# A four-layer graph transformer on one core: scatters in fours over both rankings, stages joined by chunks, and a finer wait in the sum pass

## The chip, the cores and the metric

The kernel runs on one core of one Trainium2 chip. The metric is the device time of one execution in microseconds (us). Tensors are fp32 unless marked bf16.

## The reference

The input is a graph of 3125 nodes with 256 features and 50,000 edges. Each of four layers is a graph part, a linear or softmax attention part and a mixture of experts, added to `x`. What the change touches is this, in short:

```python
# linear attention (layers 0 and 3), per head of 32 columns
q, k = elu(x @ Wq) + 1, elu(x @ Wk) + 1
ctx, den = k.T @ (x @ Wv), k.sum(nodes)             # "context"
msg = (q @ ctx) / (q @ den) @ Wo

# graph part of layer 2
agg = segment_sum(msgs[src, rel], dst)              # "sum pass"
i, f, g, o = split(agg @ W_ih.T + b_ih + b_hh)
hn = sigmoid(o) * tanh(sigmoid(i) * tanh(g))
x += relu(relu(hn @ W1.T + b1) @ W2.T + b2) @ W3.T + b3

# graph part of layer 3: this twice, with 4 heads and an elu behind it, then with 1
xW = x @ W                                          # a row per node, "table"
e = leaky_relu((xW * a_src).sum(head)[src] + (xW * a_dst).sum(head)[dst])
out = segment_softmax(e, dst) weighted sum of xW[src], + bias
```

## The kernel before

The 3125 nodes are 25 tiles of 128 (`NT`), the edges are 400 tiles of 128 (`ET`) in 50 batches of 8 (`SB`). Activations lie transposed in SBUF as `x[128, 2, 3200]`; dense work goes over them in 8 chunks of 400 columns (`CW`, `NC`), work by rows in the 25 tiles. The program is a row of stages. At the end of each all engines meet at a barrier. Inside a stage each engine has an instruction stream of its own, in the order of the code; semaphores tie them (`wait_ge`, `then_inc`).

**`rank`, the first stage.** It sorts the edges by destination (order 0, "dst") and then by source (order 1, "src"). For each order it prepares one-hot matrices, and then its ranking loop runs over 50 batches: PE counts and picks (the semaphore `chosen[o]` says how many batches it has picked, plus 2), ACT copies the counts and forms differences of keys, DVE compares and sums (its first instruction on the picks is line 318), and every second batch DVE writes the destinations of 16 edge tiles (`placed`, line 338). POOL scatters each edge tile of order 0 to DRAM with one indirect DMA, 400 in all (`scatter_slots`, line 499): 8 of a batch as soon as its two batches are placed. Order 1's 400 scatters (line 518) are spread over later stages of layer 0, beside other work: `beside=lambda pool: later.some(pool, 3)` issues three for each step.

**Small stages.** `turn_rows` (`L0_add`, `L2_turn`, `L3_h_turn`, `L3_add`) transposes 25 tiles of rows on PE and adds or copies them into `x`. `layers` and `gates` run dense layers by chunks; `context` goes over 25 tiles with key and value products, an elu and an outer product. `rows_of` makes the table of layer 3: for each tile 4 matmuls give 256 columns in PSUM; DVE copies them to a row, multiplies them with `a_src` and `a_dst` and reduces three times (lines 3780 to 3787), and SP stores the row. `finish_softmax` (`L3a_finish`, `L3b_finish`) joins the own edge of each node to the sums in `acc` on DVE, with operations over all 25 tiles. `flow` is a stage of several units that go over the chunks one behind another: in step `i` each engine does, unit by unit, the chunk `i - lag` of the unit.

**The sum pass of layer 2 (`L2_edges`).** 52 batches of 8 edge tiles. POOL gathers 128 rows for each tile (line 676) into a ring of 4 batches (`RING`), PE multiplies them with a one-hot matrix (line 688, semaphore `summed`), DVE adds the result to `acc` (line 728, `merged`); ACT makes the one-hot matrices. The softmax attention of layer 2 runs beside it. POOL waits before each batch:

```python
if n >= RING:
    pool.wait_ge(summed, (n - RING + 1) * SB)
```

## Time and profile before

| | us |
|---|---|
| median of 3 runs (7988.39 to 7998.42) | 7996.3 |
| the profiled execution, its own time | 7963.28 |
| its span | 7961.3 |
| `rank` | 996.7 |
| `L0_add`, queries, context | 144.9 |
| `L2_edges` | 701.6 |
| `L2_turn`, `L2_gates`, `L2_head` | 142.5 |
| `L3_norm`, context of layer 3 | 132.6 |
| `L3a_table` | 61.6 |
| `L3a_finish`, `L3_h_turn`, `L3_elu`, `L3b_table` | 126.7 |
| `L3b_finish`, `L3_add`, `L3_norm2` | 115.1 |

PE is TensorE, with its weight loads apart as PEld; DVE is VectorE, ACT ScalarE, POOL GpSimd, SP the engine that issues direct DMAs. The stages named are cut at their barriers; the mean clock granted to TensorE over the span is 0.812 of full speed. A busy share over the whole program says little here, since the stages have different limits.

### The profile page before, as it was taken

How to read it: one execution, taken by the hardware profiler on the slowest of the kernel's cores; microseconds unless marked ns; L12 is line 12 of the kernel's file. 1: busy time of each engine (PE TensorE's matmuls, PEld its weight loads, DVE VectorE, ACT ScalarE, POOL GpSimd, SP SyncE). 2: the span in 40 equal slices, each digit the busy share in tenths (PEclk: the TensorE clock that was granted, in tenths of full speed). 3: DMA queues.
4: the chain of work that ended last, by engine and by line, in shares of the span. 5: the costliest groups of instructions: out<-in, count | busy, mean ns of one | idle time of the engine just before them, and what ended most of it. 6: DMA issues, size and time to landing. Idle time of an engine off the chain costs nothing. (4 is left out here: it accounts for less than half of the span.)

```text
span 7961.3 us, 86418 instructions
## 1 busy us (share of the span) xinstructions
PE 5473.5 (69%) x21790; PEld 3563.2 (45%) x21790; DVE 3893.7 (49%) x9476; ACT 2872.1 (36%) x7916; POOL 3239.0 (41%) x3257
## 2 busy tenths in 40 slices
PE   2222535566799777776894668799858866888767
PEld 1111323334455455554463344555545543555544
DVE  5335835554311389994543323412456675545611
ACT  4223627774122144440112333122246642555211
POOL 3664035553466256661005652200056633555211
PEclk9999966668799878887997778699856656788588
DMA  2221521111010255550012321100034333333222
GB/s 81 66 66 40 181 71 39 41 40 17 26 33 20 70 156 159 159 146 16 8 35 86 85 82 40 39 33 30 15 101 108 106 69 86 93 88 93 56 91 86
DMA packets 270423, 568.85 MB, mean 71 GB/s; under 512 B 85678, under 2 KB 136802, under 8 KB 263906
## 3 DMA queue, kind: packets, MB, share of 16 engines
q0 software_dynamic: 134496, 314.63, 15.8%
q1 hardware_dynamic: 135554, 249.89, 9.6%
q8 instruction: 155, 2.54, 0.1%
q14 instruction: 218, 1.79, 0.1%
HBM read 519.26 MB, written 45.00 MB: 71 GB/s over the span
## 5 line engine op out<-in xcount | busy, mean ns | idle before, releaser
L1291 POOL DMA_INDIRECT L_edges_rows<-scratch_L_kv,L_edges_index x416 | 521.1, 1253 | 312.3 <-PE L_edges_ps_sum L1567 186.2
L1291 POOL DMA_INDIRECT L3a_edges_rows<-scratch_L3a,L3a_edges_index x416 | 442.9, 1065 | 446.8 <-DMA L3a_edges_last<-order_dst_last 216.5
L1291 POOL DMA_INDIRECT L3b_edges_rows<-scratch_L3b,L3b_edges_index x416 | 397.5, 955 | 465.0 <-PE L3b_edges_ps_sum L1567 302.0
L1291 POOL DMA_INDIRECT L_edges_rows<-scratch_L,L_edges_index x416 | 410.6, 987 | 320.2 <-DVE L_edges_msg L1338 176.7
L499 POOL DMA_INDIRECT scratch_by_dst<-dst_record,dst_dest x400 | 414.6, 1036 | 303.8 <-DVE dst_dest L338 185.5
L1745 POOL TENSOR_TENSOR L_norm_u_half<-x 128x400 f32<-128x400 f32 x64 | 70.8, 1109 | 1135.2 <-DVE x L1845 626.3
L676 POOL DMA_INDIRECT L_edges_rows<-scratch_L,L_edges_index x416 | 394.9, 949 | 325.1 <-PE L_edges_ps_sum L688 135.9
L518 POOL DMA_INDIRECT scratch_by_src<-src_record,src_dest x400 | 387.7, 969 | 255.1 <-issue 107.6
L688 PE MATMUL L_edges_ps_sum<-L_edges_rows,L_edges_hot 128*128 128x256 f32 x832 | 268.4, 464 | 220.4 <-issue 101.3
L400 PE MATMUL rank_ps_count<-rank_parts,rank_ident_b 128*128 128x225 bf16 x200 | 53.6, 370 | 530.9 <-DVE rank_parts L312 457.0
L1432 DVE TENSOR_TENSOR L_acc<-L_edges_ps_sum,L_acc 128x264 f32 (+1 forms) x832 | 360.0, 433 | 112.8 <-DVE L_acc L1432 56.6
L2788 DVE TENSOR_TENSOR L_experts_gated_h<-L_experts_hidden,L_experts_share_rows 128x800 f32<-128x800 f32 x112 | 111.1, 993 | 619.5 <-ACT L_experts_hidden L2778 583.8
L2778 ACT ACTIVATE L_experts_hidden<-L_experts_ps_h,L_eb_sb 128x400 f32<-128x400 f32 x320 | 187.9, 594 | 619.9 <-PE L_experts_ps_h L2740 473.1
L1567 PE MATMUL L3a_edges_ps_sum<-L3a_edges_rows,L3a_edges_hot 128*128 128x264 f32 x832 | 379.5, 618 | 0.7 <-DVE L_acc L1432 0.7
L728 DVE TENSOR_TENSOR L_acc<-L_edges_ps_sum,L_acc 128x256 f32 x416 | 176.7, 425 | 385.6 <-DMA L_edges_last<-order_src_last 196.9
L2751 PE MATMUL L_experts_ps_o<-L_experts_gated_h,L_e_sb 128*128 128x400 f32 x896 | 337.1, 518 | 29.0 <-DVE L_experts_gated_h L2788 29.0
L464 ACT ACTIVATE rank_apart<-x,rank_key_f 128x128 bf16<-128x128 f32 x800 | 244.4, 388 | 300.0 <-remote 226.7
L1567 PE MATMUL L3b_edges_ps_sum<-L3b_edges_rows,L3b_edges_hot 128*128 128x258 f32 x832 | 337.2, 557 | 4.3 <-DVE L_acc L1432 4.2
L1567 PE MATMUL L_edges_ps_sum<-L_edges_rhs,L_edges_hot 128*128 128x264 f32 x832 | 335.9, 553 | 5.5 <-DVE L_acc L1432 1.9
L2740 PE MATMUL L_experts_ps_h<-xn,L_e_sb 128*128 128x400 f32 x896 | 323.6, 505 | 2.1 <-PEq L113 2.1
L1666 ACT ACTIVATE L_edges_rhs<-L_edges_msg,L_edges_rhs 128x64 f32<-128x64 f32 x1248 | 306.6, 334 | 27.5 <-issue 21.6
L688 PEld LDWEIGHTS L_edges_ps_sum<-L_edges_rows,L_edges_hot 128*128 128x128 f32 x832 | 175.1, 227 | 307.9 <-issue 148.7
(762 smaller groups left out, 13309.7 us busy)
## 6 DMA issues: line engine op xcount, KB each, us to landing
x<-scratch_dst_key_rows SPq DMA_DIRECT2D x50, 512.0 KB
x<-scratch_src_key_rows SPq DMA_DIRECT2D x50, 512.0 KB
L_experts_w<-in_L_w SPq DMA_DIRECT2D x16, 1024.0 KB
L_edges_rows<-scratch_L,L_edges_index POOLq DMA_INDIRECT x832
L_edges_lo_rows<-order_src_lo_rows SPq DMA_DIRECT2D x52, 256.0 KB
L3a_edges_lo_rows<-order_dst_lo_rows SPq DMA_DIRECT2D x52, 256.0 KB
L3b_edges_lo_rows<-order_dst_lo_rows SPq DMA_DIRECT2D x52, 256.0 KB
x<-scratch_dst_lo_rows SPq DMA_DIRECT2D x50, 256.0 KB
```

The source lines that it names most:

```text
L464: ins = nc.scalar.activation(apart[:, u, k, :], key_line[:, u, k * P:(k + 1) * P], ACT.Abs, scale=-1.0, bias=key_f[:, ds(n * SB + k, 1)])
L499: pool.indirect_dma_start(order["table"], bass.IndirectOffsetOnAxis(order["dest"][:, t:t + 1], 0), order["record"][:, t, :], None).then_in ...
L518: pool.indirect_dma_start(self.order["table"], bass.IndirectOffsetOnAxis(self.order["dest"][:, t:t + 1], 0), self.order["record"][:, t, :] ...
L676: pool.indirect_dma_start(rows[:, n % RING, k, :], None, row_table, bass.IndirectOffsetOnAxis(index[:, t:t + 1].bitcast(U32), 0)).then_inc ...
L688: nc.tensor.matmul(ps_sum[:, k % 4, 0:F], hot[:, n % RING, k, :], rows[:, n % RING, k, :], start=True, stop=True).then_inc(summed, 1)
L1291: pool.indirect_dma_start(rows[:, n % RING, k, 0:RW], None, row_table, bass.IndirectOffsetOnAxis(index[:, t:t + 1].bitcast(U32), 0)).then_ ...
L1432: v.tensor_tensor(a, ps_sum[:, (c * SB + k) % BANKS, 0:M], a, ALU.add).then_inc(merged, 1)
L1567: nc.tensor.matmul(ps_sum[:, (c * SB + k) % BANKS, 0:M], hot[:, c % RING, k, :], values(c)[:, k, :], start=True, stop=True).then_inc(summe ...
L1666: ins = nc.scalar.activation(out, src, ACT.Copy, scale=parts(c)[:, k, h, V:V + 1])
L2740: ins = nc.tensor.matmul(ps_h[:, (a + o) % 4, 0:CW], weights[l][:, e, f, o * P:(o + 1) * P], r, start=f == 0, stop=f == len(src) - 1)
L2751: nc.tensor.matmul(ps_o[:, o, 0:CW], weights[hid][:, e, f, o * P:(o + 1) * P], gated_h[:, n % 2, f, :], start=e == 0 and f == 0, stop=False)
L2778: nc.scalar.activation(hidden[l][:, n % 2, o, :], ps_h[:, a % 4, 0:CW], func, bias=biases[l][:, n % EX, o:o + 1]).then_inc(taken, 1)
```

## The change

1. `scatter_slots` issues the 400 scatters of order 0 four at a time, one group behind each of the 100 ranking batches of both orders, where it waits for `chosen[o]`.
2. In the sum pass POOL waits for `summed` before each tile, for the tile that held the same place in the ring.
3. Layer 0: transpose and add, queries and context are one `flow`; three scatters of order 1 for each of the 25 tiles stand beside it, where 24 and 50 stood.
4. Layer 2: transpose, gates and the three dense layers are one `flow`.
5. Layer 3: norm, queries and context are one `flow`.
6. The tables of layer 3: the scores come as 8 (or 2) further columns of the matmul, whose weights are formed once from `W` and `a` (`ScoreColumns`); DVE has three copies for each tile.
7. `L3a_finish`, transpose, elu and the second table are one `flow`: `Finish` works tile by tile, and its own rows are loaded in 8 pieces.
8. `L3b_finish`, transpose, add, norm and rows are one `flow`.

```diff
-                scatter_slots(pool, orders[0], scattered, placed[0])
...
+                scatter_slots(pool, orders[0], scattered, placed[0], chosen)
...
+def scatter_slots(pool, order, scattered, placed, chosen):
...
-    for n in range(rounds):
-        if placed is not None and n % 2 == 0:
-            pool.wait_ge(placed, n // 2 + 1)
-        if n >= 4:
-            pool.wait_ge(scattered[n % 4], n // 4 * (16 * SB))
-        for k in range(SB):
-            t = n * SB + k
-            pool.indirect_dma_start(order["table"], bass.IndirectOffsetOnAxis(order["dest"][:, t:t + 1], 0),
-                                    order["record"][:, t, :], None).then_inc(scattered[n % 4], 16)
+    portion = SB // 2
+    for o in range(2):
+        for n in range(rounds):
+            pool.wait_ge(chosen[o], n + 3)
+            first = (o * rounds + n) * portion
+            b = first // SB
+            if first % SB == 0:
+                if b % 2 == 0:
+                    pool.wait_ge(placed, b // 2 + 1)
+                if b >= 4:
+                    pool.wait_ge(scattered[b % 4], b // 4 * (16 * SB))
+            for t in range(first, first + portion):
+                pool.indirect_dma_start(order["table"], bass.IndirectOffsetOnAxis(order["dest"][:, t:t + 1], 0),
+                                        order["record"][:, t, :], None).then_inc(scattered[b % 4], 16)
...
-                    if n >= RING:
-                        pool.wait_ge(summed, (n - RING + 1) * SB)
                     for k in range(SB):
                         t = n * SB + k
+                        if n >= RING:
+                            pool.wait_ge(summed, (n - RING) * SB + k + 1)
                         pool.indirect_dma_start(
                             rows[:, n % RING, k, :], None, row_table,
                             bass.IndirectOffsetOnAxis(index[:, t:t + 1].bitcast(U32), 0)).then_inc(gathered[n % RING], 16)
...
         for t in begun(i - self.lag):
+            to = self.x[:, :, t * P:(t + 1) * P]
+            got = self.ps[:, t % self.depth, 0:2 * P].rearrange("p (f n) -> p f n", f=2)
+            if self.how == "elu":
+                dve.wait_ge(self.lowered, t + 1)
+                for f in range(2):
+                    ins = v.tensor_scalar(to[:, f], got[:, f], self.bias[:, f:f + 1], 0.0, ALU.add, ALU.max)
+                ins.then_inc(self.floored, 1)
+                dve.wait_ge(self.floored, t + 1)
+                dve.wait_ge(self.raised, t + 1)
+                v.scalar_tensor_tensor(out=to, in0=self.power[:, t % 2], scalar=-1.0, in1=to, op0=ALU.add,
+                                       op1=ALU.add).then_inc(self.taken, 1)
...
+class Finish:
...
+        for t in begun(i):
+            dve.wait_ge(self.weighed, t + 1)
+            if H > 1 and t >= self.RING:
+                dve.wait_ge(self.reader.turned, t - self.RING + 1)
+            for h in range(H):
+                ins = v.scalar_tensor_tensor(out=self.out(t)[:, h * (V - 1):(h + 1) * (V - 1)],
+                                             in0=acc[:, t, h * V:h * V + V - 1],
+                                             scalar=fall[:, 0, t, h:h + 1], in1=self.own[:, t, h * V:h * V + V - 1],
+                                             op0=ALU.mult, op1=ALU.add)
+            ins.then_inc(self.finished, 1)
...
+class ScoreColumns:
...
+    def tensor(self, pe, i):
...
+            for o in range(2):
+                ins = self.nc.tensor.matmul(self.ps[:, f, :], self.w_rows[:, o, f * P:(f + 1) * P], self.a_heads[:, o, :],
+                                            start=o == 0, stop=o == 1)
+        ins.then_inc(self.made, 1)
+
...
+class Context:
...
+    def pool(self, pool, i):
+        for t in self.mine(i) if self.beside else ():
+            pool.wait_ge(self.made, t + 1)
+            self.beside(pool)
...
+            if t >= 2:
+                pe.wait_ge(self.taken, t - 1)
+            for w, at_ in ((self.wk, 0), (self.wv, D)):
+                for f in range(2):
+                    ins = self.nc.tensor.matmul(self.ps[:, t % 2, at_:at_ + D], self.src[:, f, t * P:(t + 1) * P], w[:, f, :],
+                                                start=f == 0, stop=f == 1)
+            ins.then_inc(self.made, 1)
+            if t >= 1:
+                self.outer(pe, t - 1)
...
     attention_out(kit, f"{name}_out", q, ctx, den, spread, wo, dst, floor, plus, shrink, bias, besides[1])


...
         (wq, wk, wv, wp, bp, spread), mix_in = m.room("L0_wq", "L0_wk", "L0_wv", "L0_wp", "L0_bp", "spread")
-        turn_rows(kit, "L0_add", rows, x, add=True, loads=mix_in)
-        q = m("L0_mix_q", [P, 2, NP])
-        layers(kit, "L0_mix_queries", [Layer(wq, xn, q, func="elu1")], beside=lambda pool: later.some(pool, 3))
-        linear_attention(kit, "L0_mix", m, xn, q, wk, wv, wp, spread, x, 1e-6, 0.0, 1.0, bias=bp,
-                         besides=(lambda pool: later.some(pool, 2), lambda pool: later.some(pool, 6)))
+        linear_attention(kit, "L0_mix", m, [TurnIn(rows, x, 0, None)], xn, wq, wk, wv, wp, spread, x, 1e-6, 0.0, 1.0, bias=bp,
+                         loads=mix_in, besides=(lambda pool: later.some(pool, 3), lambda pool: later.some(pool, 6)))
...
-                turn_rows(kit, "L2_turn", acc, agg, loads=gates_in + head_in)
                 hn = m2("L2_hn", [P, 2, NP])
-                gates(kit, "L2_gates", agg, wih, bih, hn)
-                h1, h2 = m2("L2_head_h1", [P, 1, CW]), m2("L2_head_h2", [P, 1, CW])
-                layers(kit, "L2_head", [Layer(w1, hn, h1, bias=b1, func="relu"), Layer(w2, h1, h2, bias=b2, func="relu"),
-                                        Layer(w3, h2, x, bias=b3, add=True)])
+                turned = TurnIn(acc, agg, 0, None, how="copy", depth=2)
+                gates = Gates(wih, bih, agg, hn, 1, turned)
+                first = Dense([(w1, agg[:, 1:2, :], b1)], hn, 2, gates, func="relu", banks=1)
+                second = Dense([(w2, agg[:, 0:1, :], b2)], agg[:, 1:2, :], 3, first, func="relu", banks=1)
+                third = Dense([(w3, x, b3)], agg[:, 0:1, :], 4, second, func="add", banks=1)
+                flow(kit, "L2_head", [turned, gates, first, second, third], loads=gates_in + head_in)
...
                 nc.vector.tensor_copy(row[:, 0:F].rearrange("p (h v) -> p h v", h=heads)[:, :, 0:V - 1],
                                       banks[0][:, 0:D].rearrange("p (h v) -> p h v", h=heads))
-                nc.vector.tensor_tensor(prod[:, 0, :], banks[0][:, 0:D], a_src, ALU.mult)
-                link(nc.vector.tensor_tensor(prod[:, 1, :], banks[0][:, 0:D], a_dst, ALU.mult))
-                both = prod[:].rearrange("p a (h v) -> p (a h) v", h=heads)
-                nc.vector.tensor_reduce(row[:, F:F + heads], both[:, 0:heads], X, ALU.add)
-                nc.vector.tensor_reduce(s_src[:, ds(t, 1), :].squeeze(1), both[:, 0:heads], X, ALU.add)
-                return nc.vector.tensor_reduce(s_dst[:, ds(t, 1), :].squeeze(1), both[:, heads:2 * heads], X, ALU.add)
...
-            rows_of(kit, f"{name}_table", [(src, w, D)], finish, sink=sink, setup=setup)
+                nc.vector.tensor_copy(row[:, F:F + heads], banks[0][:, D:D + heads])
+                return nc.vector.tensor_copy(both[:, t, :], banks[0][:, D:D + 2 * heads])
+
+            def sink(sp, t, r, u, extra):
+                return sp.dma_start(node_rows(table, t), extra["row"][:, u, :])
+
+            columns = ScoreColumns(w_rows, a_heads, w[:, :, D:])
+            units, src, loads = ahead(m2, weights_in)
+            flow(kit, f"{name}_table", units + [columns, Rows([[(src, w, D + 2 * heads)]], finish, 2 if units else 0,
+                                                              units[-1] if units else None, sink=sink, setup=setup, depth=3,
+                                                              columns=columns)], loads=loads)
...
-        finish_softmax(kit, f"{name}_finish", acc, heads, V, acc[:, :, 0:D], own_score=own, own_dram=table)
...
             norm = Norm(x, xn, after=skip)
-            flow(kit, "L3_norm", [skip, norm, Dense([(wq, q, None)], xn, 2, norm, func="elu1")], loads=mix_in,
-                 loads_later=weights_in + biases_in)
-            linear_attention(kit, "L3_mix", m3, xn, q, wk, wv, wm, spread, msg, -3e38, 1e-6, float(N))
-        return xn
+            linear_attention(kit, "L3_mix", m3, [skip, norm], xn, wq, wk, wv, wm, spread, msg, -3e38, 1e-6, float(N),
+                             normed=True, loads=mix_in, loads_later=weights_in + biases_in)
+        return [], xn, []
...
     with Memory(kit) as m:
         acc = m("L3_acc", [P, NT, 264])
         rows = acc[:, :, 0:D]
-        attend(kit, "L3a", 1, 4, first, order, scratch["L3a"], acc)
+        own = m("L3a_own", [P, NT, 4]), m("L3b_own", [P, NT, 1])
...
-        attend(kit, "L3b", 2, 1, between, order, scratch["L3b"], acc, lambda s: MessageMlp(kit, s, xn, msg, x))
-        turn_rows(kit, "L3_add", rows, x, add=True, bias=gb2)
+            finish = Finish(acc, 4, 65, own[0], scratch["L3a"])
+            finish.reader = TurnIn(None, h, 1, finish, how="elu", bias=gb1)
+            return [finish, finish.reader], h, weights_in
+
+        attend(kit, "L3b", 2, 1, between, order, scratch["L3b"], acc, own[1], lambda s: MessageMlp(kit, s, xn, msg, x))
+        given = msg.rearrange("p f n -> p (f n)").rearrange("p (t d) -> p t d", t=NT)
...
+            (gw,), gate_in = m2.room("L3_gw")
...
+            turned = TurnIn(rows, x, 1, done, bias=gb2, depth=2)
+            skip = AddIn(x, xn, bias=out_b, lag=2, after=turned)
+            norm = Norm(x, xn, lag=5, after=skip)
+            flow(kit, "L3_norm2", [done, turned, skip, norm,
+                                   Rows([[(xn, gw, EXPERTS), (xn, None, D)]], finish, 7, norm, depth=3),
+                                   Blank(scratch["given"][0:EXPERTS * CAPT * P, :])],
+                 loads=gate_in + bias_in)
     with Memory(kit) as m:
```

POOL, the scatters of `rank` (the name in brackets is the semaphore waited for). Before, at its start:

```order
L499 DMA scratch_by_dst<-dst_record,dst_dest 54448x8 x15
L499 DMA scratch_by_dst<-dst_record,dst_dest 54448x8 [waits rank_placed0]
L499 DMA scratch_by_dst<-dst_record,dst_dest 54448x8 x15
L499 DMA scratch_by_dst<-dst_record,dst_dest 54448x8 [waits rank_scattered0,rank_placed0]
L499 DMA scratch_by_dst<-dst_record,dst_dest 54448x8 x7
```

Now, where POOL passes from order 0's batches to order 1's:

```order
L504 DMA scratch_by_dst<-dst_record,dst_dest 54448x8 [waits rank_chosen0]
L504 DMA scratch_by_dst<-dst_record,dst_dest 54448x8 x3
L504 DMA scratch_by_dst<-dst_record,dst_dest 54448x8 [waits rank_scattered1,rank_chosen1]
L504 DMA scratch_by_dst<-dst_record,dst_dest 54448x8 x3
L504 DMA scratch_by_dst<-dst_record,dst_dest 54448x8 [waits rank_chosen1]
L504 DMA scratch_by_dst<-dst_record,dst_dest 54448x8 x3
```

Runs of 16 and 8 have become runs of 4, each behind a wait, and half of them stand beside order 1.

DVE, the second table of layer 3 (`L3b_table`; `ps` is PSUM). Before, one tile:

```order
L3780 COPY L3b_table_row<-L3b_table_ps 128x256
L3782 TENSOR_TENSOR L3b_table_prod<-L3b_table_ps,L_as_sb 128x256
L3783 TENSOR_TENSOR L3b_table_prod<-L3b_table_ps,L_ad_sb 128x256
L3785 TENSOR_REDUCE L3b_table_row<-L3b_table_prod 128x1
L3786 TENSOR_REDUCE L3b_ssrc<-L3b_table_prod 128x1
L3787 TENSOR_REDUCE L3b_sdst<-L3b_table_prod 128x1
```

Now, the end of one step of the joined stage and the start of the next (`u_rows` are the finished rows, `u_power` the exponentials of the elu):

```order
L2117 TENSOR_SCALAR L_h<-L3b_table_u_ps,L_gb_sb 128x128 x2
L2121 SCALAR_TENSOR_TENSOR L_h<-L3b_table_u_power,L_h 128x2x128
L4076 COPY L3b_table_row<-L3b_table_u_ps 128x256
L4078 COPY L3b_table_row<-L3b_table_u_ps 128x1
L4079 COPY L3b_both<-L3b_table_u_ps 128x2
...
L2282 SCALAR_TENSOR_TENSOR L3b_table_u_rows<-L_acc,L3b_table_u_fall,L3b_table_u_own 128x64 x12
L2117 TENSOR_SCALAR L_h<-L3b_table_u_ps,L_gb_sb 128x128 x2
```

The finish of one chunk (12 operations for three tiles), the turn and elu of the chunk before and the table rows of the one before that now stand in one DVE stream without a barrier between them.

## Rows read from the trace of the kernel before

**Rows 1.** The page: span, and busy time of each engine (x instructions).
```profile
span 7961.3 us, 86418 instructions
...
PE 5473.5 (69%) x21790; PEld 3563.2 (45%) x21790; DVE 3893.7 (49%) x9476; ACT 2872.1 (36%) x7916; POOL 3239.0 (41%) x3257
```

**Rows 2.** Windows of `rank`: stretch and length, busy us of the engines, clock, DMA.
```profile
8.80:96.00 87.20, 22.26 (x430) 17.21 (x431) 75.15 (x363) 54.38 (x150) 0.00 (x0) 1.00 0.25 79
96.00:676.00 580.00, 123.30 (x1288) 82.35 (x1286) 185.94 (x447) 134.39 (x435) 381.77 (x367) 1.00 0.22 66
676.00:790.00 114.00, 22.50 (x434) 17.49 (x434) 74.28 (x351) 53.40 (x150) 32.80 (x34) 1.00 0.08 25
790.00:1005.50 215.50, 122.78 (x1285) 82.17 (x1282) 181.56 (x448) 134.54 (x434) 0.00 (x0) 1.00 0.54 172
```

**Rows 3.** Waits, 96 to 676: total us, how many, longest us.
```profile
DVE x L318 <- remote: 335.2, 21, 26.7
...
POOL scratch_by_dst L499 <- DVE dst_dest L338: 185.5, 12, 105.2
```

**Rows 4.** Timeline of POOL: start us, duration us, instruction, idle time before it.
```profile
307.17 0.97 POOL L499 DMA_INDIRECT scratch_by_dst<-dst_record,dst_dest  x1 [6.72 <-DVE dst_dest L338]
...
349.04 0.97 POOL L499 DMA_INDIRECT scratch_by_dst<-dst_record,dst_dest  x1 [0.30 <-issue]
356.99 0.97 POOL L499 DMA_INDIRECT scratch_by_dst<-dst_record,dst_dest  x1 [6.99 <-DVE dst_dest L338]
```

**Rows 5.** Timeline of DVE in the same stretch.
```profile
323.80 0.57 DVE L318 TENSOR_TENSOR x<-rank_ps_pick,xn 128x400 f32<-128x400 f32 x1 [4.52 <-issue]
...
353.67 0.57 DVE L318 TENSOR_TENSOR x<-rank_ps_pick,xn 128x400 f32<-128x400 f32 x1 [26.20 <-remote]
```

**Rows 6.** Windows: `L0_add`, queries, context; then `L3_norm` and the context of layer 3.
```profile
1881.00:1900.60 19.60, 14.66 (x50) 7.29 (x50) 12.11 (x50) 0.00 (x0) 10.00 (x25) 0.50 0.31 107
1900.60:1942.30 41.70, 26.89 (x64) 12.83 (x64) 9.19 (x16) 16.65 (x32) 23.08 (x24) 0.91 0.02 2
1942.30:2025.90 83.60, 61.82 (x304) 51.61 (x304) 21.16 (x58) 19.45 (x50) 47.98 (x50) 0.93 0.02 2
...
5520.30:5589.10 68.80, 52.71 (x208) 33.74 (x208) 33.96 (x48) 39.90 (x60) 18.33 (x16) 0.83 0.11 39
5589.10:5652.90 63.80, 58.27 (x304) 52.00 (x304) 21.36 (x58) 20.02 (x50) 0.00 (x0) 0.94 0.00 1
```

**Rows 7.** Windows: the three stages of layer 2 (4898.9 on), and `L3a_table`.
```profile
4898.90:5041.40 142.50, 117.87 (x322) 60.30 (x322) 48.36 (x99) 43.92 (x64) 9.95 (x25) 0.88 0.03 8
...
5718.50:5780.10 61.60, 36.93 (x100) 22.29 (x100) 54.47 (x151) 0.00 (x0) 0.00 (x0) 0.74 0.16 55
```

**Rows 8.** Windows: `L3a_finish` to `L3_elu`; `L3b_table`; `L3b_finish` with `L3_add`; `L3_norm2`.
```profile
6498.70:6563.80 65.10, 16.11 (x50) 7.26 (x50) 54.43 (x79) 6.00 (x3) 10.00 (x25) 0.50 0.19 59
6563.80:6625.40 61.60, 37.02 (x100) 22.70 (x100) 54.44 (x151) 0.00 (x0) 0.00 (x0) 0.75 0.16 54
7456.40:7504.90 48.50, 15.95 (x50) 7.34 (x50) 37.51 (x64) 0.24 (x1) 10.00 (x25) 0.52 0.21 68
7504.90:7571.50 66.60, 60.47 (x294) 53.15 (x294) 39.87 (x90) 10.18 (x17) 18.61 (x17) 0.55 0.16 64
```

**Rows 9.** The sum pass, `L2_edges`: its window.
```profile
4197.30:4898.90 701.60, 415.96 (x1392) 285.23 (x1392) 243.56 (x565) 237.15 (x580) 394.87 (x416) 0.77 0.29 79
```

**Rows 10.** The sum pass: waits of POOL.
```profile
POOL L_edges_rows L676 <- PE L_edges_ps_sum L688: 135.9, 26, 7.9
POOL L_edges_rows L676 <- issue: 117.8, 385, 0.5
```

**Rows 11.** The sum pass: timeline of POOL over one cycle of two batches.
```profile
4324.27 0.95 POOL L676 DMA_INDIRECT L_edges_rows<-scratch_L,L_edges_index  x1 [6.80 <-PE L_edges_ps_sum L688]
...
4343.23 0.95 POOL L676 DMA_INDIRECT L_edges_rows<-scratch_L,L_edges_index  x1 [0.30 <-issue]
4350.96 0.94 POOL L676 DMA_INDIRECT L_edges_rows<-scratch_L,L_edges_index  x1 [6.78 <-PE L_edges_ps_sum L688]
```

More of the change, by code:

```diff
@@ L1887, in tensor @@
                 pe.wait_ge(*self.loaded)
-            if o == 0:
+            if o == 0 and self.after:
                 self.after.ready(pe, c)
@@ L1935, in open @@
         self.nc, self.kit, self.loaded = kit.nc, kit, loaded
-        self.ps = [s.ps(f"{name}ps{j}", [P, self.depth, 512]) for j in range(len(self.parts[0]))]
+        self.widths = [n for _, _, n in self.parts[0]]
+        self.one_bank = sum(self.widths) <= 512
+        self.ps = [s.ps(f"{name}ps{j}", [P, self.depth, 512]) for j in range(1 if self.one_bank else len(self.widths))]
         self.made, self.taken, self.chain = (s.sem(f"{name}{n}") for n in ("made", "taken", "chain"))
@@ L1939, in open, with bank @@
         self.extra = self.setup(s) if self.setup else None
+    def bank(self, j, k):
+        if not self.one_bank:
+            return self.ps[j][:, k % self.depth, :]
+        at_ = sum(self.widths[:j])
+        return self.ps[0][:, k % self.depth, at_:at_ + self.widths[j]]
     def mine(self, i):
@@ L1968, in tensor @@
             for j, (src, w, n) in enumerate(self.parts[r]):
[L1969 removed]
+                to = self.bank(j, k)
                 for f in range(src.shape[1]):
@@ L3083, in linear_attention @@
-def linear_attention(kit, name, m, xn, q, wk, wv, wo, spread, dst, floor, plus, shrink, bias=None, besides=(None, None)):
+def linear_attention(kit, name, m, ahead, xn, wq, wk, wv, wo, spread, dst, floor, plus, shrink, bias=None, normed=False,
+                     loads=(), loads_later=(), besides=(None, None)):
+    q = m(f"{name}_q", [P, 2, NP])
     ctx, den = m(f"{name}_ctx", [P, 2, D]), m(f"{name}_den", [P, 2, DEN + HEADS * NC])
-    context(kit, f"{name}_context", xn, wk, xn, wv, 2, ctx, True, den=den, scale=1.0 / shrink, beside=besides[0])
+    normed, lag = (ahead[-1], ahead[-1].last + 1) if normed else (None, 0)
+    flow(kit, f"{name}_context",
+         ahead + [Dense([(wq, q, None)], xn, lag, normed, func="elu1"),
+                  Context(xn, wk, wv, ctx, den, 1.0 / shrink, lag, normed, besides[0])], loads, loads_later)
@@ L3758, in layer2, with attend @@
         experts(kit, "L2_experts", xn, x, [e1, e2], [eb1], eb2, comb_t, scratch["shares"], ACT.Gelu)
-def attend(kit, name, j, heads, src, order, table, acc, guest=None):
+def attend(kit, name, j, heads, ahead, order, table, acc, own, guest=None):
     nc = kit.nc
@@ L3855, in layer3 @@
         rows = acc[:, :, 0:D]
[L3856 removed]
+        own = m("L3a_own", [P, NT, 4]), m("L3b_own", [P, NT, 1])
+        attend(kit, "L3a", 1, 4, first, order, scratch["L3a"], acc, own[0])
         def between(m2, weights_in):
             h = m2("L3_h", [P, 2, NP])
[L3860 to L3864 removed]
```

397 lines of the change are left out of this document (294 added, 103 removed).

## The prediction

> **What bounds the kernel now.** I read the page first: PE is busy 69% of the span and no engine more [rows 1], so no single engine is the limit. The windows cut at the barriers then give each stage its own limit. The reader should look there for two things. In `rank` the same work stands twice: the ranking loop of order 0 takes 580.0 us, that of order 1 215.5 us, with the same busy times on PE (123.3 and 122.8), DVE (185.9 and 181.6) and ACT (134.4 and 134.5) and the clock at 1.00 in both [rows 2]. The only difference is POOL, which scatters in the first and not in the second. So some 364 us of waiting come with 400 scatters. In the small stages the busiest engine fills 70 to 95% of a stage that is 20 to 85 us long, and the rest is fill, drain and a clock of 0.50 to 0.56 where PE has little to do [rows 6 to 8].
>
> The waits name the loss in `rank`: DVE's first instruction on PE's picks waits 335.2 us for "remote", 21 times, up to 26.7 us, and POOL waits 185.5 us for destinations [rows 3]. The timeline shows how: POOL scatters 32 tiles back to back from 307.17 to 349.04 + 0.97 = 350.01 and then waits 6.99 us [rows 4]; DVE's line 318 comes at 323.80 after an idle time of 4.52 us, which began at 323.80 - 4.52 - 307.17 = 12.1 us into the run, and the next one at 353.67 after 26.20 us, only 3.7 us after the last scatter has ended [rows 4, 5]. So for some 12 us of a run the other engines keep their pace, then they nearly stand, and 3.7 us after POOL stops they go on. POOL itself is limited to one scatter in 1.28 us: 32 in 42.8 us, and a few of them longer [rows 4].
>
> **Rank (part 1).** The 400 scatters stay, so POOL still has 400 x 1.28 = 512 us of them. A group of four is 5.1 us, a ranking batch alone 215.5 / 50 = 4.3 us. So POOL is now the slower of the two, and both loops go at its pace or slower. How much slower is not in the trace, for no run of four stands there. From below: 5.1 us a batch, 510 for both loops. From above: the disturbance per scatter stays what it is, 364.5 / 400 = 0.91 us, and the loops take 2 x 215.5 + 364.5 = 795.5, as now. POOL can run at most about two groups ahead, since each waits for a batch picked; after some 12 us of scatters the other engines slow, no pick comes, POOL stops, and they recover in up to 3.7 us. I take that as a cycle of three batches, 15.3 us of scatters and 2.5 us of stop, 17.8 / 3 = 5.9 us a batch, 590 for 100. A second estimate agrees: with scatters beside it a tile of `context` takes 83.6 / 25 = 3.34 us and without 63.8 / 25 = 2.55, which is 0.40 us for each of 50 scatters [rows 6]; 431 + 400 x 0.40 = 591. So the loops lose 795.5 - 590 = 205 us. Order 1's preparation takes 114.0 us with scatters still draining into it (34 of them), order 0's takes 87.2 without [rows 2]; now at most one group is left there: -27. The last groups come behind order 1's last picks and must land: +8. Sum **-224**, bounds -304 (5.1 us a batch) and about -19 (nothing but the gap).
>
> The Trainium skill, SBUF — State Buffer, section "Who interferes with whom", says that PE and ACT never wait on anyone and that a DMA never contends with a compute engine. By it there would be no disturbance for a new schedule to remove, and `rank` would gain the gap alone; this trace does not agree, with 580.0 against 215.5 us for equal work.
>
> **Joined stages (parts 3 to 8).** For each I take the busiest engine over the joined windows, PE's at a better clock where it had been starved, plus some 5 us of ends (the context of layer 3 takes 63.8 for 58.3 of PE [rows 6]). The upper bound of each is today's time, for the work is nearly the same; the lower is that engine's own time.
> - Layer 0: 144.9 now. PE has 14.7 us at clock 0.50 in the turn (7.3 at full clock), 26.9 in the queries, and 58.3 in a context without scatters: 92.5, with ends 98; 75 scatters at 0.40 add up to 30, and I take two thirds of it, since some now fall beside the turn and the queries: 118, **-27** (98 to 135).
> - Layer 2: 142.5 now, PE 117.9 of it [rows 7], of which the turn, as in `L0_add`, is 14.7 at clock 0.50 [rows 6]; at full clock 110.6 and ends of 7: 118, **-25** (112 to 142).
> - Layer 3's norm, queries and context: 68.8 + 63.8 = 132.6; PE 52.7 + 58.3 = 111.0, with ends 116: **-17** (111 to 132).
> - `L3a_table`: 61.6, bound by DVE's 54.5 us in 151 operations of which half go [rows 7]; about 27 of DVE and 36.9 of PE stay. What takes over is PE at clock 0.74 or the round trip of the row stores with two buffers, which no row prices apart; between 37 and 61.6 I take the middle, 48: **-14**.
> - Finish, turn, elu and second table: 65.1 + 61.6 = 126.7. DVE's 54.4 + 54.4 = 108.9 [rows 8] lose the half of the table's (27), and the turn's copies, since the elu now reads PSUM (12, by `L0_add`'s DVE time for 25 tiles [rows 6]): 70. Ahead of the first tile stand the finish's chain over all tiles and the loads of the own rows, and the lags of two chunks at clock 0.50: 18. Together 88: **-39** (70 to 115).
> - Finish, add, norm and rows: 48.5 + 66.6 = 115.1; PE 16.0 + 60.5 = 76.4 at clocks 0.52 and 0.55, DVE 37.5 + 39.9 = 77.4 [rows 8]. The two lie beside each other; 77 and 15 for head and lags of seven chunks: 92, **-23** (80 to 112).
>
> Sum **-145**, range -90 to -190.
>
> **Sum pass (part 2).** It takes 701.6 / 52 = 13.5 us a batch [rows 9], in cycles of two batches: 16 gathers back to back in 19.9 us, then 6.8 us of waiting for the eighth sum of the batch that holds the ring [rows 11]. POOL waits 135.9 us so, 26 times [rows 10]. With a wait for each tile POOL starts again seven sums earlier, and a sum is two matmuls, 2 x 416.0 / 1392 = 0.6 us of PE [rows 9], so some 4 us of the 6.8. But what held the sums up is the run of gathers itself, as in `rank`, and only the stop lets them go on; an earlier start brings the next stall earlier. POOL's floor is (394.9 + 117.8) / 52 = 9.9 us a batch. I take 12.6 us a batch, a quarter of the way: **-45**; bounds 0 and -146 (POOL without a stop, 513 + 42 of ends = 555).
>
> **The sum.** -224 - 145 - 45 = -414. The profiled execution takes 7963.3, 33 less than the median of the three runs; against the median the forecast is 7996.3 - 414 = **7582**.
>
> **Rivals.**
> - The forecast (0.50): short runs avoid most of the stand. Its own range is 7500 to 7680: `rank` -290 to -150, the joins -170 to -110, the sum pass -90 to 0, not all at one end.
> - The cost goes by the scatter, not by the run (0.25). For it: in `context` 2 scatters a tile still cost 0.40 us each, with pauses between runs of 8 [rows 6]. Against it: line 318 waited 4.5 us in the first 17 us of the run and 26 us after that [rows 5], which a cost per scatter would not give. Then `rank` gains 19, the sum pass nothing: 7996 - 19 - 145 = 7832. The Trainium skill's rule on who interferes with whom (SBUF — State Buffer) would end at the same number.
> - Nearly no stand is left (0.20): `rank` at POOL's pace, -304, the sum pass -146, the joins -145: 7996 - 595 = 7401.
> - Slower than before (0.04): order 1's loop is free of scatters today. If every group stalls PE, DVE and ACT for as long as it lasts and they recover only behind it, a batch costs 5.1 + 3.5 + up to 4.3 = 12.9 us in both orders, 1290 against 795.5, +495, and with the gap and the joins +323: 8319. It decides from (795.5 + 27 + 145) / 100 = 9.7 us a batch on. Against it: runs of 8 in `context` leave PE 61.8 of 83.6 us busy [rows 6].
>
> Within 0.2% (16 us, about what a measurement of this kernel can tell from no change) only a batch of 9.5 to 9.8 us would end: 0.01. Faster 0.95, slower 0.04. The range is 7420 to 7800: it holds the forecast's case, the nearer part of the third and that part of the second in which the sum pass or a join gives some 30 us more than I count; what lies beyond, and the slower case, is about 2 in 10.
>
> **What would show it.** `rank` should be 765 to 780 us long, both loops alike at about 295 us, waits for "remote" short and many instead of 26 us long, and POOL in runs of 8 to 12 scatters with pauses. If it is wrong by the second case, order 1's loop has grown by as much as order 0's has shrunk. Each joined stage should show PE or DVE above 80% of its window and a clock above 0.6; one that stands at its old sum has a wait in the DVE stream, most likely for the own rows or the stores. In the sum pass the stops of POOL should be shorter and more. The forecast fails most easily in the 5.9 us a batch: 1 us there is 100 us.

## The result, and the profile after

The changed kernel takes 7622.39 us (median of 4 runs, 7620.41 to 7626.74), the kernel before 7992.35 (7977.42 to 7998.42) in the same comparison: ratio 0.954, 95% interval 0.9524 to 0.9557, or -370 us. The forecast was 7582, with a range of 7420 to 7800.

The page of the changed kernel gives its span and the busy times that answer to [rows 1]:

```profile
span 7624.5 us, 84609 instructions
## 1 busy us (share of the span) xinstructions
PE 5477.4 (72%) x21806; PEld 3599.0 (47%) x21806; DVE 3788.4 (50%) x9408; ACT 2917.8 (38%) x8107; POOL 3185.7 (42%) x3157
```

The span fell from 7961.3 by 336.8 us. That is less than 370, since the profiled execution of before was 29 us under the median of its four, and that of the changed kernel 4 us above its own. The windows of the changed kernel, cut at its barriers (the columns are those of [rows 2]), show `rank` in four pieces (preparation and loop of order 0, then of order 1). Behind them stand, in the order of the program, the joined stage of layer 0, the sum pass, the joined stage of layer 2, norm to context of layer 3, `L3a_table`, finish to second table, and finish to rows:

```profile
9.00:97.00 88.00, 23.12 (x439) 17.92 (x440) 76.32 (x366) 54.94 (x151) 0.00 (x0) 1.00 0.26 79
97.00:404.50 307.50, 122.52 (x1281) 81.78 (x1279) 184.46 (x441) 134.40 (x433) 219.53 (x197) 1.00 0.40 123
404.50:483.00 78.50, 23.92 (x455) 18.64 (x455) 73.88 (x357) 54.02 (x152) 3.37 (x3) 1.00 0.11 35
483.00:797.60 314.60, 121.49 (x1264) 80.97 (x1261) 184.22 (x446) 134.10 (x432) 224.06 (x200) 1.00 0.40 120
...
1681.30:1811.70 130.40, 93.13 (x418) 72.63 (x418) 38.81 (x99) 35.73 (x82) 71.82 (x75) 0.85 0.07 18
...
3982.50:4670.20 687.70, 422.49 (x1392) 290.18 (x1392) 243.12 (x565) 237.44 (x580) 393.61 (x416) 0.76 0.30 80
...
4670.20:4798.60 128.40, 105.49 (x322) 57.18 (x322) 43.91 (x74) 35.83 (x57) 0.00 (x0) 0.97 0.03 9
5281.60:5398.90 117.30, 105.66 (x512) 82.49 (x512) 54.23 (x106) 59.21 (x110) 17.68 (x16) 0.91 0.07 23
5463.70:5500.40 36.70, 27.64 (x108) 20.04 (x108) 14.80 (x77) 0.00 (x0) 0.00 (x0) 0.94 0.26 93
6221.90:6307.60 85.70, 49.94 (x158) 33.29 (x158) 60.80 (x264) 48.52 (x176) 0.00 (x0) 0.71 0.26 84
7135.90:7236.20 100.30, 72.16 (x344) 61.34 (x344) 68.24 (x176) 20.56 (x43) 18.61 (x17) 0.56 0.21 75
```

| part | before | after | difference | forecast |
|---|---|---|---|---|
| `rank` | 996.7 | 788.7 | -208.0 | -224 |
| layer 0, joined | 144.9 | 130.5 | -14.4 | -27 |
| layer 2, joined | 142.5 | 128.4 | -14.1 | -25 |
| layer 3, norm to context | 132.6 | 117.3 | -15.3 | -17 |
| `L3a_table` | 61.6 | 36.6 | -25.0 | -14 |
| finish to second table | 126.7 | 85.7 | -41.0 | -39 |
| finish to rows | 115.1 | 100.3 | -14.8 | -23 |
| sum pass | 701.6 | 687.8 | -13.8 | -45 |
| all that the change doesn't touch | | | +9.6 | 0 |

The last line is mostly layer 0's edge pass: 770.8 before, 784.1 after with the same instructions, and 776.9, 778.9, 778.8 and 784.5 in the four kernels of experiments 1 to 4, none of which changes its instructions. So I take it for spread between executions.

What `rank` does now is seen on POOL. Its timeline shows one cycle of eight scatters:

```profile
313.12 0.97 POOL L504 DMA_INDIRECT scratch_by_dst<-dst_record,dst_dest  x1 [1.15 <-remote]
314.39 0.97 POOL L504 DMA_INDIRECT scratch_by_dst<-dst_record,dst_dest  x1 [0.30 <-issue]
315.67 1.85 POOL L504 DMA_INDIRECT scratch_by_dst<-dst_record,dst_dest  x1 [0.30 <-issue]
...
325.37 0.96 POOL L504 DMA_INDIRECT scratch_by_dst<-dst_record,dst_dest  x1 [1.10 <-remote]
```

Two groups go back to back, POOL stops for 1.1 us, and the cycle is 325.37 - 313.12 = 12.25 us for two batches. DVE in the same stretch (line 318, as in [rows 5]) waits 3.1 us in each second batch instead of 26.20 in each fourth:

```profile
313.00 0.57 DVE L318 TENSOR_TENSOR x<-rank_ps_pick,xn 128x400 f32<-128x400 f32 x1 [3.14 <-remote]
316.94 0.57 DVE L318 TENSOR_TENSOR x<-rank_ps_pick,xn 128x400 f32<-128x400 f32 x1 [0.27 <-PE rank_ps_pick L413]
...
325.25 0.57 DVE L318 TENSOR_TENSOR x<-rank_ps_pick,xn 128x400 f32<-128x400 f32 x1 [3.10 <-remote]
```

The waits of the whole of `rank`, to be held against [rows 3] (total us, how many, longest):

```profile
DVE x L318 <- remote: 158.3, 50, 7.4
```

### The profile page after: what moved, and what is told of

The parts are those of the page before. It is cut to its first block and busy times, and to the rows that moved or that the text cites. A ratio compares the mean times of both kernels' runs of the same rounds, so it can differ in the third digit from the quotient of the medians.

```text
span 7624.5 us, 84609 instructions
## 1 busy us (share of the span) xinstructions
PE 5477.4 (72%) x21806; PEld 3599.0 (47%) x21806; DVE 3788.4 (50%) x9408; ACT 2917.8 (38%) x8107; POOL 3185.7 (42%) x3157
## 5 line engine op out<-in xcount | busy, mean ns | idle before, releaser
L1296 POOL DMA_INDIRECT L_edges_rows<-scratch_L_kv,L_edges_index x416 | 481.9, 1158 | 353.3 <-PE L_edges_ps_sum L1572 236.3
L504 POOL DMA_INDIRECT scratch_by_dst<-dst_record,dst_dest x400 | 447.0, 1117 | 339.3 <-issue 107.7
L681 POOL DMA_INDIRECT L_edges_rows<-scratch_L,L_edges_index x416 | 393.6, 946 | 308.4 <-PE L_edges_ps_sum L693 110.1
L1635 ACT ACTIVATE L_edges_hot<-iota,L_edges_lo 128x128 f32<-128x128 f32 x832 | 265.0, 388 | 126.0 <-issue 70.6
L1572 PE MATMUL L_edges_ps_sum<-L_edges_rows,L_edges_hot 128*128 128x272 f32 x832 | 310.4, 506 | 3.2 <-DVE L_edges_rows L1419 3.2
```

What stands on the lines that cost most here:

```text
L504: pool.indirect_dma_start(order["table"], bass.IndirectOffsetOnAxis(order["dest"][:, t:t + 1], 0), order["record"][:, t, :], None).then_in ...
L681: pool.indirect_dma_start(rows[:, n % RING, k, :], None, row_table, bass.IndirectOffsetOnAxis(index[:, t:t + 1].bitcast(U32), 0)).then_inc ...
L1296: pool.indirect_dma_start(rows[:, n % RING, k, 0:RW], None, row_table, bass.IndirectOffsetOnAxis(index[:, t:t + 1].bitcast(U32), 0)).then_ ...
L1572: nc.tensor.matmul(ps_sum[:, (c * SB + k) % BANKS, 0:M], hot[:, c % RING, k, :], values(c)[:, k, :], start=True, stop=True).then_inc(summe ...
L1635: ins = nc.scalar.activation(hot[:, c % RING, k, :], kit.iota[:], ACT.Abs, scale=-1.0, bias=lo[:, ds(n * SB + k, 1)])
```

## The experiments

The experiments ran in four groups, each on one chip: P (1 to 4), Q (5 and 7 to 9), R (10 and 11) and S (6 and 12). The kernel before was timed beside each group, and its time fell into two kinds: 7992 us in the comparison above, 7969 on chip P and 7898 on chip R, but 7072 on chip Q and 7071 on chip S. Each ratio below is to the kernel before on the same chip. I call 7898 to 7992 us the first kind of chip and 7071 to 7072 the second. The two kinds turned out to be the finding of the study.

**1. The old order of scatters in the changed kernel.** (Chip P, before 7969.0.)

```diff
-            pool.wait_ge(chosen[o], n + 3)
-            first = (o * rounds + n) * portion
...
+        if n % 2 == 0:
+            pool.wait_ge(placed, n // 2 + 1)
+        if n >= 4:
+            pool.wait_ge(scattered[n % 4], n // 4 * (16 * SB))
+        for k in range(SB):
```

> The changed kernel with the old order of scatters (8 of a batch behind its placing, all beside order 0). If the new order of scatters gave what the stages of the two traces differ by, rank goes back from 788.7 to about 997 us and the whole from 7622 to 7830. If a cost per scatter were unchanged and the 208 us came from elsewhere, it stays within 30 us of 7622.

Measured: 7816.1 us (4 runs), ratio 0.9808 (0.9776 to 0.984); `rank` 997.3 us long. With the changed kernel's 788.7, the gain in `rank` is that of the scatters' order. What is left of the change, 153 us against before, are the joins and the sum pass; the table above has 124.6 + 13.8 = 138 for them.

**2. Spread over both orders, but in runs of 32.** (Chip P.)

```diff
-    for o in range(2):
-        for n in range(rounds):
-            pool.wait_ge(chosen[o], n + 3)
+    for g in range(0, 2 * rounds, 8):
+        pool.wait_ge(chosen[g // rounds], g % rounds + 3)
+        for b in range(g // 2, min(g // 2 + 4, rounds)):
...
+            for t in range(b * SB, (b + 1) * SB):
```

> The 400 scatters still spread over both ranking loops, but 32 in a row behind every eighth batch instead of 4 behind each. Theory A (long unbroken runs make the other engines stand, short ones avoid it): a run of 32 is 41 us, in which about 3 batches are ranked in the first 12 us and nearly none in the rest, then 3.7 us of recovery and 5 batches at 4.3 us: 66 us for 8 batches, 8.3 a batch, rank about 1000 us, the whole about +210. Theory B (what counts is only that POOL's 512 us now lie beside both loops, whatever the runs): 41 us of scatters for 8 batches stays POOL's pace or slower by little, 5.3 to 6.2 a batch, rank 700 to 790 us, the whole between -90 and 0 us from 7622.

Measured: 7846.81 us, ratio 0.9846 (0.9819 to 0.9873), +226 us against the 7620.45 of experiment 4 on the same chip, which has the changed kernel's time; `rank` is 1019.9 us. Theory A. POOL in this kernel over one cycle of eight batches:

```profile
169.18 0.97 POOL L500 DMA_INDIRECT scratch_by_dst<-dst_record,dst_dest  x1 [21.41 <-PE rank_ps_pick L413]
...
210.63 0.97 POOL L500 DMA_INDIRECT scratch_by_dst<-dst_record,dst_dest  x1 [0.30 <-issue]
237.74 0.97 POOL L500 DMA_INDIRECT scratch_by_dst<-dst_record,dst_dest  x1 [26.14 <-PE rank_ps_pick L413]
```

and, in it, DVE and the last of PE's eight picks (line 413) between DVE's two:

```profile
184.10 0.57 DVE L318 TENSOR_TENSOR x<-rank_ps_pick,xn 128x400 f32<-128x400 f32 x1 [5.88 <-remote]
186.92 0.20 PE L413 MATMUL rank_ps_pick<-rank_parts,xn 128*128 128x50 bf16 x1
215.31 0.57 DVE L318 TENSOR_TENSOR x<-rank_ps_pick,xn 128x400 f32<-128x400 f32 x1 [27.53 <-remote]
```

The run lasts from 169.18 to 211.6. After 184.10 DVE starts on no pick until 215.31, 3.7 us behind the run's end, though by the trace PE had the pick ready at 187.12. Then five batches go at their own pace until 237.7. The cycle is 68.6 us where the theory had 66. So spreading over both orders is worth nothing by itself here: what counts is how long a run is.

**3. No scatters in `rank`.** (Chip P, one execution. The table by destination keeps its blanks, so the sums by destination are empty; `rank` alone is read.)

```diff
-    for o in range(2):
-        for n in range(rounds):
...
+    pool.wait_ge(placed, rounds // 2)
+    pool.wait_ge(chosen[1], rounds + 2)
```

> No scatters of order 0 at all: the table of edges by destination holds only its blanks, so later edge passes by destination sum nothing; rank alone is read. Both loops at the 4.3 us a batch that order 1 showed alone: 215 + 215, with the preparations 88 and 78, rank about 600 us. What is over this in the changed kernel (about 190 us) is what 400 scatters still cost, 0.47 us each; the prediction had 0.40.

Measured: `rank` is 593.1 us. The windows of its two loops:

```profile
97.00:310.00 213.00, 122.92 (x1282) 82.10 (x1282) 180.73 (x445) 134.43 (x433) 0.00 (x0) 1.00 0.54 174
387.00:600.00 213.00, 122.27 (x1281) 81.59 (x1278) 179.48 (x440) 134.09 (x433) 0.00 (x0) 1.00 0.55 174
```

The changed kernel's 400 scatters still cost 788.7 - 593.1 = 195.6 us, 0.49 us each.

**4. Two batches of lead for POOL.** (Chip P.)

```diff
-            pool.wait_ge(chosen[o], n + 3)
+            pool.wait_ge(chosen[o], n + 1)
```

> Each group of four may go two batches earlier (8 scatters of lead). Theory A (pauses in POOL's stream let the others recover; at 6.15 us a batch POOL already runs 92% of the time): no gain, the steady state is POOL's pace of 5.1 us plus its longer scatters (8 in 11.2 us) and a pause of about 1 us, so at most -0.5 us a batch, and more likely 0 to +40 us in all, because runs become longer before the pause. Theory C (POOL only waits too long for the picks, so the wait is the limit): 5.6 us a batch, -50 us.

Measured: 7620.45 us, ratio 0.9553 (0.9526 to 0.958), the changed kernel's 0.954; `rank` is 789.5 us. POOL comes to the same run of eight and the same stop of 1.1 us. The last pick before the stop, and POOL's first scatters of two runs:

```profile
308.44 0.20 PE L413 MATMUL rank_ps_pick<-rank_parts,xn 128*128 128x50 bf16 x1
312.15 0.96 POOL L504 DMA_INDIRECT scratch_by_dst<-dst_record,dst_dest  x1 [1.08 <-remote]
324.47 0.97 POOL L504 DMA_INDIRECT scratch_by_dst<-dst_record,dst_dest  x1 [1.06 <-remote]
```

In both kernels POOL starts a run 3.5 us after PE has made the pick that the code waits for; counted through the trace, here it is the pick of two batches before the one of the changed kernel. So POOL uses its lead once and then stops at the same wait again. The pace is that of the picks, and how far POOL may run ahead of them does not change it. Theory A, and C falls.

**5 and 6. The finer wait of the sum pass alone, in the kernel before.** (Chips Q and S, before 7071.75 and 7070.91.) The edit is the sum pass's part of the diff.

> The kernel before with the finer wait of the sum pass alone. By the prediction -45 us (12.6 us a batch); by the stages of the two traces -14 us (701.6 to 687.8). If sums are held up by the gathers themselves, POOL's pauses are only cut into smaller ones and the gain stays at 0 to -20.

> The kernel before with the finer wait of the sum pass alone, once more, since on the chip of the first try POOL never waited in that pass. On a chip with the hold-up: the stages say -14 us, 0.2%; the prediction said -45. On a chip without: 0 again.

Measured: 7072.29 us, ratio 1.0005 (0.9996 to 1.0014), and 7066.54, ratio 0.9995 (0.9982 to 1.0008). Both chips were of the second kind, so this tells nothing of the first, where the wait alone was not run. But the trace of the first shows what that kind is. Its windows: the two ranking loops, with the old order of scatters, and the sum pass:

```profile
96.00:311.00 215.00, 122.79 (x1282) 81.99 (x1280) 187.35 (x440) 134.45 (x433) 163.42 (x142) 1.00 0.54 175
390.00:606.00 216.00, 121.73 (x1271) 81.34 (x1268) 186.32 (x437) 133.71 (x433) 169.38 (x154) 1.00 0.60 174
...
3585.00:4130.50 545.50, 383.27 (x1392) 279.69 (x1392) 242.42 (x565) 237.05 (x580) 393.75 (x416) 0.86 0.38 101
```

Its waits from 96 to 606 have no row with "remote", and these of POOL:

```profile
POOL scratch_by_dst L499 <- issue: 108.2, 355, 0.3
POOL scratch_by_dst L499 <- DVE dst_dest L338: 104.1, 1, 104.1
```

All 400 scatters run back to back from 104.6 to 662 us, and beside them order 0's loop takes 215 us instead of the 580.0 of [rows 2]. The gathers of the sum pass hardly stop either (no wait of POOL for a sum is longer than 0.3 us): 545.5 us instead of 701.6 [rows 9].

**7 and 8. POOL 24 or 16 gathers ahead of the sums instead of 32.** (Chip Q.) The edit, for 16:

```diff
-                        if n >= RING:
-                            pool.wait_ge(summed, (n - RING) * SB + k + 1)
+                        if t >= 16:
+                            pool.wait_ge(summed, t - 16 + 1)
```

> The changed kernel with POOL at most 24 gathers ahead of the sums instead of 32. Theory A (unbroken runs of gathers hold up PE and DVE): runs get shorter, and since PE needs only 8 tiles to be there, the pass gets no longer, perhaps 10 to 30 us shorter. Theory D (the pass needs the depth, because PE and DVE must work while POOL waits): 10 to 40 us longer.

> The same with 16 ahead, two batches. Theory A: POOL is held to the pace of the sums, runs of 8 or less, the pass 20 to 60 us shorter than 687.8. Theory D: the gather of a batch no longer hides behind the sums of the one before, 30 to 100 us longer.

Measured: 6949.18 us, ratio 0.9826 (0.9807 to 0.9845), and 6942.59, ratio 0.9823 (0.9807 to 0.9839); the sum pass is 547.0 and 547.2 us. On this kind of chip the depth does nothing, so both theories, A and D, missed: there was no hold-up to test them on. These two, with a wait that does nothing here, stand for the changed kernel on this kind: about -125 us, not -370. Their `rank` is 674.5 and 672.3 us against 664.3 in experiment 5 on the same chip: here the new order of scatters gives nothing, and costs 8 to 10 us. On chip S it is 673 us in experiment 12 against 670.3 in experiment 6.

**9. The joined stage of layer 0 without scatters beside it.** (Chip Q; they go to the experts' stage and what finds no room there to a stage of its own.)

```diff
-                         loads=mix_in, besides=(lambda pool: later.some(pool, 3), lambda pool: later.some(pool, 6)))
+                         loads=mix_in, besides=(None, lambda pool: later.some(pool, 6)))
```

> The joined stage of layer 0 without the 75 scatters beside it (they move to the experts' stage, six a step as there, whose 64 steps have room for them). By the prediction's terms the joined stage takes 98 us instead of the measured 130.5 (92.5 of PE and 5.5 of ends). What the experts' stage pays for 75 more is open: at the 0.40 us of the context it is +30 and the whole stays, if they hide behind its matmuls the whole gains 30.

Measured: 7014.11 us, ratio 0.9919 (0.9904 to 0.9935), 65 and 71 us slower than the two kernels before it. The joined stage with scatters (24 ahead, first fence) and without (second):

```profile
1348.00:1466.00 118.00, 85.63 (x418) 68.73 (x418) 38.92 (x99) 36.69 (x82) 72.02 (x75) 0.85 0.08 20
```

```profile
1349.20:1446.20 97.00, 85.71 (x418) 68.81 (x418) 38.91 (x99) 36.68 (x82) 0.00 (x0) 0.92 0.07 22
```

97 us, as the prediction's terms said (98). My count of the room elsewhere was wrong: the experts' stage grew by only 8 us (407.0 to 415.1), but its steps took only their six each, and the rest stood alone for some 89 us.

**10. The changed kernel again, and, 11 and 12, gathers paced.** (Chip R, before 7898.01; the last one on chip S, before 7070.91.) Besides the 16 of experiment 8:

```diff
-                    if n >= RING and kind == "dual":
-                        pool.wait_ge(used, n - RING + 1)
+                    if n >= 2 and kind == "dual":
+                        pool.wait_ge(used, n - 1)
```

> The changed kernel once more, for the chip. Two kinds of chip have shown so far: one on which the kernel before takes 7969 us and long runs of scatters hold up the other engines, one on which it takes 7072 us, POOL never stops and no engine waits for remote. On the first kind the ratio is 0.954 as in the first comparison. On the second kind rank was 664 us before and 672 to 675 in kernels with the new scatters, the sum pass 546 in both, so only the joined stages remain: about -125 us, ratio 0.983.

> The changed kernel with gathers held to 16 tiles ahead of the sums in the sum pass, and to two batches ahead of their use in the edge pass of layer 0. On a chip where POOL's runs hold up the others: if runs of 8 with short pauses are better than runs of 16 with long ones, as in rank, the pass of layer 0 falls from about 780 us to 620 to 700 and the sum pass from 688 to 600 to 670; if the depth is what the passes need, both grow by 30 us or more. On a chip without the hold-up, where POOL runs through at about 565 and 547 us: no change, or a little longer if two batches are too few.

> The changed kernel with gathers held to 16 tiles (sum pass) and two batches (edge pass of layer 0) ahead, once more. On a chip with the hold-up the ratio to before is 0.949 as on the last one, about 0.004 below the changed kernel's. On a chip without it, 0.983, the changed kernel's by its stages, or up to 0.002 more if two batches ahead are too few there.

Measured: the changed kernel 7534.29 us (7521.31 to 7551.27), ratio 0.9533 (0.9503 to 0.9563); paced 7505.92 (7485.34 to 7519.2), ratio 0.9493 (0.9462 to 0.9523), 28 us (0.4%) faster: the slowest paced run lies 2 us under the fastest of the other, and the intervals of the two ratios overlap. The windows of layer 0's edge pass and of the sum pass, first of the changed kernel on that chip, then paced:

```profile
876.50:1634.20 757.70, 425.59 (x1300) 279.03 (x1300) 401.18 (x1049) 533.23 (x1873) 413.14 (x416) 0.67 0.20 40
3933.00:4606.20 673.20, 421.54 (x1392) 286.87 (x1392) 243.34 (x565) 237.01 (x580) 394.80 (x416) 0.77 0.31 82
```

```profile
875.10:1612.30 737.20, 440.63 (x1300) 290.33 (x1300) 400.95 (x1049) 529.51 (x1873) 414.43 (x416) 0.65 0.21 41
3922.10:4577.40 655.30, 423.76 (x1392) 293.92 (x1392) 243.66 (x565) 237.48 (x580) 394.30 (x416) 0.77 0.31 84
```

-20.5 and -17.9 us: more than the whole difference. The sum pass landed in the range expected (600 to 670), layer 0's pass (620 to 700) did not. Why the two are shorter is open. The reason expected, shorter runs with shorter stops, is not in the traces: in layer 0's pass POOL stops 25 times instead of 26, most runs being of 16 in both kernels, and in the sum pass its stops add up to 123 us instead of 110. And each pass stands here with one execution: two stages that the edit does not touch, layer 0's experts and layer 1's edge pass, are 8 us longer in the paced trace. On chip S the paced kernel takes 6946.35, ratio 0.9822 (0.98 to 0.9844), as the others of the second kind. It has the lowest time on the first kind of chip, by little, and is no worse on the second.

## Why the prediction was right, and where it was not

**Rank: the mechanism right, the size right to 16 us.** The prediction said that long runs make the others stand and that short ones avoid most of it. Experiment 2 shows the first half apart from everything else (cycle 68.6 us against a worked-out 66), experiment 1 that the order alone gives the gain. The term of the loops was 5.9 us a batch and is 6.2: the two windows are 307.5 + 314.6 = 622 us against 590. The cycle is not three groups and a stop of 2.5 us but two groups and a stop of 1.1 us. POOL's own pace was taken too fast: among eight scatters two are longer (1.85 and 1.35 us), so the eight take 11.15 us, 5.6 a batch instead of 5.1. The prediction's own 42.8 us for 32 scatters already gave 1.34 us each. So the 5.1 a batch of the lower bound was out of reach, and the stop, 0.55 us a batch, is less than the 0.8 taken. The gap between the orders gave 114.0 - 78.5 = 35.5 us where 27 were counted, and the 8 us for the last groups did not show: order 0's preparation, the loops and the gap give all of the 208. The cross-check by 0.40 us a scatter was near too: experiment 3 measures 0.49.

**What is late is a signal.** The prediction said that the other engines "nearly stand", and left open what they stand for. The trace of before shows it. DVE's line 318 waits for `chosen[o]` alone, which PE raises with the last of its eight picks, and ACT's line 471 for the counts of PE's line 400. The last pick, and ACT's copy:

```profile
325.74 0.54 PE L400 MATMUL rank_ps_count<-rank_parts,rank_ident_b 128*128 128x225 bf16 x2 [5.48 <-issue]
326.62 0.20 PE L413 MATMUL rank_ps_pick<-rank_parts,xn 128*128 128x50 bf16 x1
337.97 0.35 ACT L471 CAST rank_parts<-rank_ps_count 128x225 bf16<-128x225 f32 x1 [11.75 <-remote]
```

By the trace the counts were done at 326.3 and the pick at 326.8, and ACT went on 11.7 us and DVE 26.9 us later [rows 5]. In the changed kernel DVE starts at 313.00 on a pick that was done at 309.55. In the trace of experiment 5, with POOL's scatters back to back, no pick waits longer than 1.0 us for DVE. So a rival that was not named, that the direct loads of the next batch come late behind the scatters, does not explain these waits. What delays the signal is in no trace; the ends of matmuls are modelled in a profile, so it is not excluded that PE itself completes them late.

**The rival of a cost by the scatter fell**: with the same 400 scatters `rank` is 788.7, 1019.9 or 997.3 us by the length of the runs. The rival of nearly full recovery and the slower one did not come: 6.2 us a batch lie between 5.1 and the 9.7 from which the change would have lost. The Trainium skill, SBUF — State Buffer, section "Who interferes with whom", says that PE and ACT never wait on anyone and a DMA never contends with a compute engine. Experiments 5 to 9 agree on two chips (215 us for the loop beside scatters without a pause; 213 without any in experiment 3, on chip P), and the traces of three comparisons on other chips do not. The section is about the ports of SBUF, and nothing here shows that the late signals have to do with these.

**The sum pass: the step that failed.** The prediction took a quarter of the way from 13.5 us a batch to POOL's 9.9, 12.6; it is 687.8 / 52 = 13.2, -13.8 us instead of -45. POOL's waits there, to be held against [rows 10]:

```profile
POOL L_edges_rows L681 <- PE L_edges_ps_sum L693: 110.1, 98, 7.3
```

98 waits instead of 26, and 110.1 us instead of 135.9: POOL starts earlier, and that brings the next hold-up earlier, as the prediction argued, but nearly in full. Even the 13.8 us are not clear of spread: the same sum pass took 683, 694 and 689 us in experiments 1, 2 and 4, and before stands here with one trace. That the hold-up and not the depth of the ring sets this pass is borne out by the second kind of chip, where the same code takes 546 us, and by the paced kernel on the first, where half the depth makes it no longer.

**The joins: -124.6 instead of -145**, each inside its bounds but `L3a_table`, which fell just below the 37 taken as PE's time at clock 0.74: 36.6. Finish to second table came within 2 us by two errors that offset each other: DVE has 60.8 us where 70 were counted, and the rest is 24.9 instead of 18. In `L3a_table`, with DVE out of the way, the clock granted was 0.94 and PE's time 27.6 us instead of 36.9; what ends DVE's waits is the row store, as named:

```profile
DVE L3a_table_row L4076 <- DMA scratch_L3a<-L3a_table_row: 14.6, 19, 1.2
```

In layer 0 the floor was right (97.0 for 98), and the scatters were under-counted: I took two thirds of 0.40 us for each of 75, 20 us; it was 130.4 - 97.0 = 33 us, 0.45 each, on the first kind of chip (the floor is from the second), and 21 us on the second. In layer 2 the ends are not 7 but 128.4 - 105.5 = 23 us. PE's waits account for 21 of them: it waits for DVE's adds of the last dense layer and for DVE's copies of the transposed tiles, and for one load:

```profile
PE L_head_u_ps L1897 <- DVE x L1928: 10.4, 9, 1.5
PE L_head_u_ps L2104 <- DVE L_agg L2126: 8.1, 9, 2.4
PE L_head_u_ps L2172 <- DMA L_b_sb<-in_L_b: 2.7, 1, 2.7
```

In finish to rows, 100.3 for 92, the prediction took 77 us of DVE and 15 of ends; PE is busy 72.2 us and DVE 68.2, and PE waits some 28 us for DVE, 9.6 of it for the first finished rows. Both causes are read from the waits alone and were not tried.

**Where the prediction was blind**: it gave one number for the change. Its rank term exists on one kind of chip only. On the other the change is worth 1.8%, the joins.

## What to carry to other kernels

Where a busy time is the same and a loop's length is not, look at what another engine does beside it, and at the length of its unbroken runs rather than at its share. Cut such runs at the point where the others begin to stand (here some 12 us). Do not count on a finer wait when the engine that is waited for is the one that is held up: here it gave 14 us of 702, hardly more than the spread. Take such a gain for what it is on more than one chip before it is counted on.

## What the runs showed of the hardware

- Beside long runs of indirect DMAs issued by POOL the other engines get PE's signals late on some chips: DVE waited up to 27.53 us for "remote" beside 32 scatters in a row, for a pick made 28.2 us before, and went on 3.7 us after them. With runs of eight it waited about 3.1 us in every second batch.
- On two other chips nothing of it was to be seen: the same kernel before took 7072 and 7071 us instead of 7898 to 7992, with the same POOL time per scatter (0.97 us and 0.30 of issue for most). What differs between the chips is open: nothing in the traces names it, and no run could choose its chip.
- Gathers go with the same difference: the sum pass takes 701.6 or 545.5 us by the chip, with 394.9 and 393.8 us of POOL. Between the traces of before and of experiment 5, whose code differs in the sum pass's wait alone, the stages in which POOL issues no indirect DMA differ by at most 5 us each, and the seven in which it issues 278 to 416 are 11 to 332 us shorter on the second kind.
